# Softmax attention whose input is normalised, turned and kept on chip by the stage before it

## The reference

```python
x = x + attn_a(_layernorm(x))   # linear attention, 16 heads of 8, then a 128-512-128 block, two norms
x = x + ffn(_layernorm(x))      # the softmax attention and the experts, below
x = x + attn_b(_layernorm(x))   # attention without softmax, 16 heads of 64
x = x + ffn(_layernorm(x))      # the same ffn again, the same weights

def _mha(x, ...):               # x is (16, 256, 128) here: the 16 rows of a batch entry attend to each other
    q, k, v = split(x @ Wqkv.T + bqkv)          # 4 heads of 32
    att = softmax(q k^T / sqrt(32))
    return (att @ v) @ Wo.T + bo

def _moe(x, ...):               # out of 8 experts the one with the largest logit
    idx = argmax(x @ Wg.T)
    return relu(x @ W1[idx] + b1[idx]) @ W2[idx] + b2[idx]

def ffn(x):
    y = norm(x + _mha(x), g1, be1)
    return norm(y + _moe(y), g2, be2)
```

## Time and profile before

| | us |
|---|---|
| Median of three runs | 657.47 (656.88 to 659.5) |
| The profiled execution | 655.18 |
| Its span | 653.5 |
| PE busy | 605.0 (93%) |
| DVE busy | 453.0 (69%) |
| ACT busy | 380.7 (58%) |
| POOL busy | 393.0 (60%) |

### The profile page before, as it was taken

How to read it: one execution, slowest core, us unless ns; L and a number is a source line. 1 busy time by engine, 2 the same in 40 slices (tenths; PEclk the granted TensorE clock), 3 DMA queues, 4 the chain that set the end, 5 groups by cost and what they waited for, 6 DMA issues and landing times.

```text
span 653.5 us, 18934 instructions
## 1 busy us (share of the span) xinstructions
PE 605.0 (93%) x5780; PEld 521.5 (80%) x5780; DVE 453.0 (69%) x2176; ACT 380.7 (58%) x974; POOL 393.0 (60%) x634
## 2 busy tenths in 40 slices
PE   8999999987999879999988999999789997999993
PEld 5889999955777659999975788887667785999993
DVE  2676677756798878988851433333669888899984
ACT  3587767648999435566523333331499973556651
POOL 4465668953488775888851212120337887587886
PEclk8999999978999999999997999999999999999998
DMA  5871000143123462333140000000512323433320
GB/s 137 306 260 46 18 18 26 42 155 84 34 82 95 123 198 66 96 93 89 56 134 13 18 25 17 24 16 25 137 36 61 90 89 95 116 99 90 85 83 23
DMA packets 58090, 53.84 MB, mean 82 GB/s; under 512 B 7851, under 2 KB 52308, under 8 KB 57676
## 3 DMA queue, kind: packets, MB, share of 16 engines
q1 hardware_dynamic: 51050, 36.19, 20.2%
q0 software_dynamic: 5568, 12.96, 5.8%
q10 hardware_dynamic: 1378, 3.55, 1.5%
HBM read 31.33 MB, written 19.83 MB: 78 GB/s over the span
## 4 chain that ended last, share of the span: by engine, by line
PE 62%; POOL 12%; DVE 10%; issue 6%; ACT 5%; DMA 3%; ACTq 1%; POOLq 1%; DVEq 0%; SPq 0%
PE bank L1584 9%; PE wide L1595 6%; POOL sorted_dram L1483 5%; PE wide L1770 5%; PE wide L1743 5%; PE wide L625 4%; PE bank L1756 4%; POOL rstd L1469 3%; PE bank L1595 3%; PE wide L642 2%; PE wide L669 2%; PE bank L678 2%; POOL rows_e L1476 2%; PE bank L1777 1%; PE wide L491 1%
## 5 line engine op out<-in xcount | busy, mean ns | idle before, releaser
L1584 PE MATMUL bank<-zt,late 128*128 128x128 f32 x624 | 84.8, 277 | 2.1 <-DVE hid_f L1646 2.0
L1584 PEld LDWEIGHTS bank<-zt,late 128*128 128x128 f32 x624 | 76.5, 192 | 4.2 <-DVE hid_f L1646 3.4
L1469 POOL TENSOR_TENSOR rstd<-var_m,half_neg 128x2 f32<-128x2 f32 (+1 forms) x50 | 40.3, 805 | 65.7 <-DVE nmean L1372 64.5
L1483 POOL DMA_INDIRECT sorted_dram<-rows_e,pos x64 | 65.3, 1021 | 19.3 <-issue 18.8
L1527 POOL TENSOR_TENSOR rstd<-var_e,half_neg 128x1 f32<-128x1 f32 x78 | 61.0, 781 | 15.9 <-DVE var_e L1655 13.7
L1607 ACT ACTIVATE late<-we 128x512 f32 x80 | 50.5, 631 | 24.3 <-PE bank L1584 20.4
L1595 PE MATMUL wide<-late,hid_f 128*128 128x128 f32 x416 | 55.1, 275 | 0.0
L1722 POOL TENSOR_TENSOR var_m<-mvs,eps 128x2 f32<-128x2 f32 x16 | 3.1, 196 | 80.0 <-DVE mvs L1823 80.0
L1595 PEld LDWEIGHTS wide<-late,hid_f 128*128 128x128 f32 x416 | 50.6, 192 | 0.1
L1534 POOL DMA_INDIRECT out<-xout,dest x39 | 40.4, 1036 | 11.2 <-issue 11.0
L1827 DVE COPY late<-wide 128x1024 f32<-128x1024 f32 x16 | 19.6, 1225 | 39.7 <-PE wide L1770 39.7
(11 more groups left out here) (300 smaller groups left out, 1815.3 us busy)
## 6 DMA issues: line engine op xcount, KB each, us to landing
rows_e<-sorted_dram SPq DMA_DIRECT2D x78, 128.5 KB, 2.1
xa<-x_dram SPq DMA_DIRECT2D x9, 640.0 KB, 6.6
we<-L_ffn_W SPq DMA_DIRECT2D x16, 256.0 KB
x_dram<-xout SPq DMA_DIRECT2D x32, 128.0 KB, 1.8
early<-late SPq DMA_DIRECT2D x128, 32.0 KB
sorted_dram<-L_attn_a_x ACTq DMA_DIRECT2D x2, 1028.0 KB
rows_e<-L_ffn_b SPq DMA_DIRECT2D x1, 1024.0 KB
hid_f<-L_ffn_b ACTq DMA_DIRECT2D x1, 1024.0 KB
```

Source lines behind the costliest of these rows:

```text
L1469: nc.gpsimd.tensor_tensor(rstd[:, c, w], var_m[:, c, w], half_neg[:, w], ALU.pow).then_inc(g["rstd"], 1)
L1483: nc.gpsimd.indirect_dma_start(sorted_dram[n][:, :], bass.IndirectOffsetOnAxis(ap=pos[:, p % 3, t:t + 1], axis=0), pay[:, p % PAYS, t, :], ...
L1584: last = nc.tensor.matmul(to[:, (m % 2) * P:(m % 2 + 1) * P], we_t[:, c1, m * P:(m + 1) * P], zt[:, c1, 0, 0:P], start=True, stop=True)
```

## The change

The norm and the turn of the attention's input move into the stage ahead of it, for both attentions.

- Stage A gets a fourth norm (statistics n3) of the rows `xout` just made, and ACT writes the normalised rows into `z_out`. PE turns them (`turn`), ACT copies them with the constant bias into `z_all` (`keep_turned`), a buffer of 128x4096 that keeps all turned rows of the stage on chip, already in the attention's order of rows. These steps are at depths 15 to 18, so they all stand in bodies 15 to 33, after the last input pair has come in.
- Beside it `y = xout + be2` is made, on POOL for pairs 0 to 5 and 13 to 15, on DVE for pairs 6 to 12, and SP stores y in place of x. `xout` gets a fourth buffer.
- Block B gets the same at depths 4 and 5: norm beside its own, y on POOL, turn on PE. Its hardware loops are written out.
- The attention loses the load of x, the statistics, the norm, the turn and its copy, and the add on POOL and DVE. It waits for the last `z_kept` and reads its operands from `z_all`. SP loads y for each pair straight into the payload, two pairs behind the probabilities.
- The first 11 weight folds stand among stage A's last bodies: seven in PE's bodies 19 to 25, four in 26 to 29; their DVE copies stand after DVE's last body. Products of ones ahead of the attentions go (4 in the first, 15 in the second); block B gets 6 ahead of its last turn.
- The first `z_all` lies where block B's weights will be, so Wo is loaded later, in the first experts; clears of `p_t`, `p_x` and `k_x` move to POOL.

```diff
+        wb_o, wk, vo = parts(room_b, (HB // 2, D), (HB * DB,), (HB, D))
+        def turned_rows(n, t, count=1):
+            return z_all[n][:, t * P:(t + count) * P]
...
+        Y_BY_DVE = range(6, PAIRS - 3)
...
+        def turn(pe, n, p):
+            after(pe, z_kept, n * PAIRS + (p if n or p < 9 else p - 1))
+            to = turned_bank(n, p)
+            for t in range(2):
+                last = nc.tensor.transpose(to[:, t * P:(t + 1) * P], z_out[n][:, p % 3, t, :], ident[:, :])
+            last.then_inc(z_turned, 1)
+        def keep_turned(act, n, p):
+            at = turned_bank(n, p)
+            act.wait_ge(z_turned, n * PAIRS + p + 1)
+            nc.scalar.activation(z_all[n][:, :].rearrange("p (l s) -> p s l", s=S)[:, p, :], at[:, 0:2 * P], ACT.Copy,
+                                 bias=HAT).then_inc(z_kept, 1)
...
-                if i == PAIRS + 7:
+                if PAIRS + 10 <= i < PAIRS + 14:
+                    n = HATS_FIRST + i - PAIRS - 10
+                    pe.wait_ge(g["r2"], PAIRS)
+                    hat_products(pe, hats_f[n:n + 1], N_A + n)
+                if has(17):
+                    p = i - 17
+                    if p == 0:
+                        pe.wait_ge(g["phi"], 2 * PAIRS)
+                    pe.wait_ge(g["z3"], p + 1)
+                    turn(pe, 0, p)
+                if PAIRS + 3 <= i < PAIRS + 3 + HATS_FIRST:
+                    n = i - PAIRS - 3
                     pe.wait_ge(w_o_in, 16 * len(loads_o))
-                    hat_products(pe, hats_f[:3], N_A)
-            pipeline(pe, PAIRS, 10, 1, body, PAIRS)
-            hat_products(pe, hats_f[3:HATS_FIRST], N_A + 3)
+                    hat_products(pe, hats_f[n:n + 1], N_A + n)
+            pipeline(pe, PAIRS, 18, 1, body, PAIRS)
...
+                if has(18):
+                    keep_turned(act, 0, i - 18)
...
+                if has(15):
+                    p = i - 15
+                    c = (p + 16) % 3
+                    act.wait_ge(g["shift"], p + 17)
+                    after(act, z_turned, p - 2)
+                    for t in range(2):
+                        last = nc.scalar.activation(z_out[0][:, p % 3, t, :], xout[:, p % 4, t, :], ACT.Identity,
+                                                    bias=shift[:, c, 6 + t:7 + t], scale=rstd[:, c, 6 + t:7 + t])
+                    last.then_inc(g["z3"], 1)
...
+                    after(dve, g["z3"], p - 3)
+                    rows_left(dve, p - 4)
...
+                if has(16):
+                    p = i - 16
+                    dve.wait_ge(g["xo"], second_of_two(p))
+                    bn([xout[:, p % 4, 0, :], xout[:, p % 4, 1, :]], p % 3, 6, g["n3"])
...
+                if has(16):
+                    p = i - 16
+                    after(dve, g["step"], p + 14)
+                    aggregate("n3", p, 6, (p + 16) % 3, None)
...
+                if i - 16 in Y_BY_DVE:
+                    p = i - 16
+                    after(dve, y_stored[p % 3], 16 * (p // 3))
+                    nc.vector.tensor_tensor(y_out[0][:, p % 3, :, :], xout[:, p % 4, :, :], b2f[:, :].unsqueeze(1)
+                                            .to_broadcast([P, 2, D]), ALU.add).then_inc(g["y3_late"], 1)
...
+                    w = slice(0 if has(0) else 2 if has(7) else 4 if has(12) else 6,
+                              8 if has(16) else 6 if has(12) else 4 if has(7) else 2)
...
+                if has(16) and i - 16 < Y_BY_DVE.start:
+                    p = i - 16
+                    after(pool, y_stored[p % 3], 16 * (p // 3))
+                    times_row(y_out[0][:, p % 3, :, :], xout[:, p % 4, :, :], b2f, ALU.add).then_inc(g["y3"], 1)
...
+            for p in range(Y_BY_DVE.stop, PAIRS):
+                pool.wait_ge(a_s["xo"], second_of_two(p))
+                after(pool, y_stored[p % 3], 16 * (p // 3))
+                times_row(y_out[0][:, p % 3, :, :], xout[:, p % 4, :, :], b2f, ALU.add).then_inc(g["y3"], 1)
+            pool.wait_ge(hat_kept, N_A + 4)
+            nc.gpsimd.memset(p_t[:, :, :, :], 0.0).then_inc(p_cleared, 1)
+            pool.wait_ge(z_turned, PAIRS)
+            nc.gpsimd.memset(p_x[:, :, :, :, :], 0.0).then_inc(k_cleared, 1)
...
-                for sem_, count in stored_before:
-                    sp.wait_ge(sem_, count)
-                x_rows = src_dram[:, :].rearrange("(t p) d -> p t d", p=P)
-                for k, (lo, hi) in enumerate(G_PARTS):
-                    sp.dma_start(xa[:, lo:hi, :], x_rows[:, lo:hi, :]).then_inc(x_back[k], 16)
...
+                    if p >= PAYS:
+                        sp.wait_ge(sorted_[p % PAYS], uses(p, PAYS, 32) - 32)
...
+                    sp.dma_start(pay[:, p % PAYS, :, D:2 * D], y_rows[:, 2 * p:2 * p + 2, :]).then_inc(y_in[p % PAYS], 16)
...
+                    if i >= 2:
+                        load_y(i - 2)
                 pipeline(sp, PAIRS, 1, 1, body, PAIRS)
+                for p in (PAIRS - 2, PAIRS - 1):
+                    load_y(p)
...
-                        if i == 1:
-                            spin(pe, WO, 1)
-                        pe.wait_ge(g["zt0"], o + p + 1)
...
-                        nc.tensor.matmul(QV[:, 0:256], wf_qkv[:, 0:D], zt_m[:, p % 6, :], start=True, stop=True)
+                        nc.tensor.matmul(QV[:, 0:256], wf_qkv[:, 0:D], turned_rows(n, 2 * p, 2), start=True, stop=True)
...
-                    if has(0):
-                        pe.wait_ge(g["z0"], o + i + 1)
-                        after(pe, g["zt0"], o + i)
-                        for t in range(2):
-                            last = nc.tensor.transpose(TT[:, t * P:(t + 1) * P], z1[:, i % 3, t, :], ident[:, :])
-                        last.then_inc(g["turned0"], 1)
...
-                    if has(1):
-                        p = i - 1
-                        act.wait_ge(g["turned0"], o + p + 1)
-                        after(act, g["wo"], o + p - 5)
-                        nc.scalar.activation(zt_m[:, p % 6, :], TT[:, 0:256], ACT.Copy, bias=HAT).then_inc(g["zt0"], 1)
...
-                    if has(0):
-                        act.wait_ge(g["shift"], ob + i + 1)
-                        after(act, g["turned0"], o + i - 2)
-                        for t in range(2):
-                            last = nc.scalar.activation(z1[:, i % 3, t, :], tile(xa, i * 2 + t), ACT.Identity,
-                                                        bias=shift[:, i % 3, t:t + 1], scale=rstd[:, i % 3, t:t + 1])
-                        last.then_inc(g["z0"], 1)
...
-                    if has(2) or has(11):
-                        c, w = (i - 2) % 3, slice(0 if has(2) else 2, 4 if has(11) else 2)
...
-                        for k in range(w.start, w.stop):
-                            last = nc.vector.bn_aggr(mvs[:, c, k, :], stats[:, (i - 2) % 3, k, :])
-                        last.then_inc(g["agg"], 1)
...
+                    if has(11):
...
+                        for k in range(2):
+                            last = nc.vector.bn_aggr(mvs[:, c, k, :], stats[:, c, k, :])
+                        last.then_inc(g["norm"], 1)
...
-                    if has(0) or has(9):
-                        w, c = slice(0 if has(0) else 2, 4 if has(9) else 2), i % 3
...
-                        nc.gpsimd.tensor_tensor(rstd[:, c, w], var_m[:, c, w], half_neg[:, w], ALU.pow).then_inc(g["rstd"], 1)
...
-                    if has(8) and i - 8 < PAY_X_BY_DVE:
-                        p = i - 8
-                        if p >= PAYS:
-                            pool.wait_ge(sorted_[p % PAYS], uses(p, PAYS, 32) - 32)
-                        nc.gpsimd.tensor_tensor(pay[:, p % PAYS, :, D:2 * D], both(xa, p),
-                                                b2f[:, :].unsqueeze(1).to_broadcast([P, 2, D]), ALU.add).then_inc(g["pay_x"], 1)
...
+                    if has(0):
...
+                        nc.gpsimd.tensor_tensor(rstd[:, c, 0:2], var_m[:, c, 0:2], half_neg[:, 0:2], ALU.pow).then_inc(g["rstd"], 1)
...
+                        pool.wait_ge(y_in[p % PAYS], uses(p, PAYS, 16))
...
+                    c, w = i % 3, slice(0 if has(0) else 2, 4 if has(4) else 2)
...
+                        p = i - 4
+                        after(pool, y_stored[p % 3], stores(p % 3) + 16 * (p // 3))
+                        nc.gpsimd.tensor_tensor(y_out[1][:, p % 3, :, :], xout[:, p % 3, :, :],
+                                                b2f[:, :].unsqueeze(1).to_broadcast([P, 2, D]), ALU.add).then_inc(g["y3"], 1)
...
+                    if has(5):
+                        if i == PAIRS + 4:
+                            spin(pe, XW, 6)
+                        pe.wait_ge(g["z3"], i - 4)
+                        turn(pe, 1, i - 5)
...
+                    if has(4):
+                        p, c = i - 4, i % 3
+                        act.wait_ge(g["shift"], i + 1)
+                        after(act, z_turned, PAIRS + p - 2)
+                        for t in range(2):
```

(5 more changed lines are left out.)

332 lines of the change are left out of this document (165 added, 167 removed).

## The result

| | before | after |
|---|---|---|
| Median of 14 runs, us | 657.82 | 650.28 |
| Ratio of the runs, 95% interval | | 0.9884 (0.9862 to 0.9906) |
| The profiled execution, us | 655.18 | 650.18 |
| Its span, us | 653.5 | 648.2 |

The change as a whole went the way that was forecast, and the attention's main term came out in size; the handovers between the stages and the drains did not.

What follows compares the result with a forecast made beforehand. PE bounds block B; POOL sets the attention's full-body beat, ACT its fill. Terms sum to -18.7 us: 655.18 profiled becomes 636.5, or 638.8 at the median of 657.47, rounded to 639; own range 634 to 644, wider 630 to 651.

Steps and rivals of the forecast that it cites:

- Attention, full bodies: Bodies 8 to 15 of each attention at 4.2 us with PE the bound, 29.4 us; bodies 4 to 8 at 14.4.
- The second rival: A round through four engines, not engine load, sets the attention's 4.5 us beat; 12.5 us gain goes: 651; chance 0.11.
- Attention, fill: First four attention bodies go from ACT's 3.15 us to 3.0 each, 12.0 us against 14.0: gain 2.0.
- Drains: Attention's drain: about four bodies at POOL's 4.37 us, falling to 3.7; gains 2.3 us in the first attention, 1.5 second.
- Block B: A turn of two tiles adds 0.22 us to some 13 full bodies of block B: +2.9 us.
- Block B's end: Last `xout` add plus 0.4, 4.0 and 0.4 us gives key product at 462.7, not 466.4: 3.7 us gained.
- Stage A: Drain: POOL falls 3.6 us behind, last `xout` add near 141.6, first key product 148.1 against 148.7: gain 0.6.
- The first rival: POOL's and PE's arrears in stage A add up, block B costs 0.45 us per pair: 646; chance 0.17.
- The rule weighed: DVE and POOL lock a shared SBUF port pair; stage A's six POOL adds could hold DVE up to 4.4 us.
- SP's queue: Attention's y loads wait for the scatter of five pairs before, ahead of the next probability transfers; costed at nothing.
- third rival: Attention's scatter lands late, y loads delay the probability transfers and PE waits: 669; chance 0.05.
- The clock: Slow start at PE's lower clock ahead of the first attention, filler products gone: 1.0 us added, bounds 0 and 3.

## Why the forecast was wrong

**Attention, full bodies: right.** From the fifth key product of the first attention to the last it took 43.9 us, against 14.4 + 29.4 = 43.8; a pair takes 4.08 us against 4.2, and PE is the bound. The two terms were off against each other (15.0 and 28.8). The reading of POOL's beat holds for the bodies of 4.69 us as far as the rows of before go; the average of 4.57 us per pair was a mixture of bodies of two lengths. No run gave POOL its whole old work back, so this reading rests on rows alone. The second rival (a round that keeps the beat) is refuted; that its 651 us is nearest to the measured 650.3 is luck.

**Attention, fill: near in size, wrong in reason.** The failed step is "ACT alone sets 3.15 us per pair": with 1.27 us of ACT's work gone the beat is 3.14. So ACT's load did not hold it, and PE's turn did not either (3.14 with the turn back); what does was not tested. What the fill gained, 1.7 and 1.3 us against 2.0, is almost all in its first step, where 1.4 had been put as an estimate.

**Drains: the step "about four bodies of it still go at POOL's 4.69 - 0.32" failed.** Behind the last key product only one body of before went at 4.37; the next took about 3.9 and more, without POOL's add, since that had gone to DVE for the last four pairs. The bodies of 4.37 lie mostly before that product, where the full bodies are counted. And the one fell to 4.08, PE's beat, not to 3.7. 1.1 and -0.1 us came in place of 2.3 and 1.5. In the second drain PE also waits 2.0 us more for the probabilities than before, a wait that was put at nothing; its part in the miss stays open.

**Block B: right.** +2.7 us from first to last `xout` (96.6 before, 99.3 after) against +2.9; a pair takes 6.93 us against 6.71.

**Block B's end: the largest miss, 4.6 us.** The failed step is the sum 0.4 + 4.0 + 0.4 = 4.8 us from the last add to the key product, where 9.4 came. It lets the new chain run from the last add and never prices the six products of ones, which the account of the change names and which stand ahead of the last turn. They are 3.3 us by the run with them placed earlier. The other 1.3 remain in that run, where the last turn still waits 1.02 us for ACT's copy of the turn before; they were not taken apart.

**Stage A: the second miss, 3.1 us.** The failed step is the size of POOL's arrears, put at 3.6 us; its last row operation came 5.5 us later. The sum left out the clear (1.38 us), which POOL does inside a body. The 2 us taken off for DVE's wait behind a fold did come: 3.06 us of idle time before, 0.51 after. So the add came 3.4 us later in place of 1.6. The clear alone is not the whole cause, since moving it gives nothing: PE's last second product starts 3.9 us later too (130.73 to 134.66), where the forecast put no number on PE. Relieving both engines gives 1.4 us, and 2.2 of the 3.6 stay open. Behind the add, 6.5 us were forecast and 8.8 came: the clock, and the folds between the turns. The first rival (upstream pays more, 646) was nearest in kind as to stage A; its price for block B (0.45 us per pair) did not come.

**The rule weighed: seen, and small.** The twelve last `xout` adds of stage A took 6.66 us on DVE before and 7.50 after, 0.84 us more, where the rule's bound was 4.4.

**SP's queue: right in full bodies.** With the y loads in it PE is busy 12.00 of 12 us, so the third rival's wait for the probabilities does not exist there. In the second drain it does, three times, 2.67 us in all.

**The clock.** I gave it 1.0 us in one place. In the profile of the changed kernel it is at its lower level in four stretches of 6.8 us ahead of the program's end, two of which the kernel before does not have (458.2 to 465.0 and 546.9 to 553.7). Where it falls, and for how long (3 to 20 us), differs between executions. The Trainium skill (TensorE: Matmul & The Clock Gate, Part 1) says that "the default state is throttled, and activity releases the throttle". The run without the products agrees in part: the clock fell at 462.6 us, when PE was busy 1.26 of 4 us (460 to 464), and was back at 1.00 in 480 to 484. In between, from 468 us on, rows show PE busy 3.07 to 3.14 of 4 us at 1.2 GHz.

## What to carry to other kernels

Where a stage's tail is already full on two engines, work moved into it makes it longer, and relieving one of the two engines shows nothing: relieve both before you judge either. An instruction in an in-order queue ahead of the last step of a chain is on the path once it outlasts the idle time that it stands in, filler products above all, since they are issued just where the clock is low; put them into the idle time before, not in front of what is waited for. Giving one engine its old work back shows that it can set a beat, not that it did: look also for bodies of the old kernel in which that engine's work is the same and the beat is not, and do not average over bodies of two kinds.

## What was not expected of the hardware

- The sum of ACT's durations overstates its load: the removed copy and two normalisations, 1.27 us by their rows, raise its busy time by about 0.9 per pair when given back (13.66 of 14 us at 4.57 per pair, against 10.60 in three), and by 0.55 when the two of 128x128 were plain copies.
- DVE's adds of two operands in stage A's drain are slow only when a row operation of POOL's is running as they start. Of the last 12 `xout` adds, 4 met one before (832 to 837 ns) and 6 after (683 to 992); they took what was left of it and about 0.28 us. All others took 359 to 461 ns, also those that began during one of POOL's powers. The run with doubled turns has 8 slow ones, though its edit touches only PE: it shifts the two against each other.
- The idle time that POOL shows ahead of an indirect DMA is partly a wait that other work can fill: 0.55 us without the add ahead of it, 0.17 with it.
